# A gated delta-rule attention block on one core: weighted k, token-major z, no identity product, small scaling products on GpSimd, new orders

## The chip, the cores and the metric

The kernel runs on one core of a Trainium2 chip. The core has a matrix engine (TensorE, PE in the profile), a vector engine (VectorE, DVE), a scalar engine (ScalarE, ACT), a general engine (GpSimd, POOL) and a queue engine that issues the DMAs (SyncE, SP). Each takes its own instructions strictly in the order in which they are written, and they wait for each other with semaphores. The metric is the device time of one execution in microseconds (us). It is quoted as a median over executions.

## The reference

One transformer layer: a modulated layer norm, linear attention with a gated delta rule, and a small mixture of experts. The change lies almost wholly in the attention. For each of 8 batches and 16 key heads (128 pairs, called steps) there are two value heads and four chunks of 128 tokens. The reference writes it in chunks of 64; the kernel works in chunks of 128. Cut to what matters:

```python
mixed = silu(conv4(x @ W.T))        # q, k: 16 heads of 128; v: 32 heads of 128; z beside them, without conv
q, k = l2norm(q), l2norm(k)          # x / (|x| + 1e-6)
beta, g = sigmoid(b), cumsum(-exp(A_log) * softplus(a + dt_bias))   # per token and value head
decay = where(tril, exp(g[:, None] - g[None, :]), 0)
A = -where(strict_tril, (k*beta) @ k.T * decay, 0)
T = inverse(eye - A)                 # per chunk and value head
for each chunk:                      # state is 128 x 128 per value head, 0 at first
    v_new = T @ v_beta - (T @ (k_beta * exp(g))) @ state
    out   = (q * exp(g)) @ state + tril(q @ k.T * decay) @ v_new
    state = state * exp(g_last) + (k * exp(g_last - g)).T @ v_new
h = out * rsqrt(mean(out*out) + 1e-6)
y = (norm_weight * h * silu(z)) @ W_out.T
```

## The kernel before

Three stages follow each other: layer norm and gates, attention, experts. The attention stage holds 128 steps, one for each pair of batch and key head. Within a step everything is 128 partitions wide; `U` = 8 is four chunks times two value heads.

The work of a step is cut into named tasks. Each engine has a string (`PE_ORDER`, `ACT_ORDER`, `DVE_ORDER`, `POOL_ORDER`) that lists its tasks for one iteration of the steady loop. `P3@4` means: task P number 3, of the step four after the iteration's own number. An iteration so holds tasks of five steps (a software pipeline), and each step passes through five iterations. The orders alone set what stands behind what on an engine; a task waits on semaphores for what it reads and for the buffers it writes.

The tasks that matter here, in a step's own sequence:

- P0 to P11 (L658): the projections, six tiles (k, q, two of v, two of z) of two half products each, 128x512 float32. C copies a tile from PSUM with the last tap as scale (ACT L886), T adds the other three taps (DVE L1018). SK, SQ and SV are silu. Z is silu of the z tiles, straight from PSUM (ACT L891).
- KT, QT, KN, QN: transposes of k and q, their squares (ACT) and the sums of squares (DVE L1024, L1028). PW takes the root (POOL L1199). SM0 to SM3 and SN0 to SN2 (DVE L1034 to L1060) make the scales from it, each on 8 or 4 elements per partition: `neg_n`, `inv` (the reciprocal), `cc`, `neg_c`, `w_c`, `q_s2`, `q_s`.
- GL and GE: `low` = row of g plus a 0 or -1e30 mask (POOL L1194), and its exponential (ACT L924). KK (PE) is k.k and k.q, GA (DVE L1072, 8 instructions) multiplies it by `neg_c` and the decay. SL (POOL L1203) writes -1 into the diagonal, AR and AL split the matrix into bf16 parts, AB (DVE L1078) copies its diagonal blocks to `a_bd`.
- L, M, q, y, X, XB, Y: six levels of a blockwise inverse in bf16. On each level PE makes a product M, DVE masks it (q), DVE transposes `y_h` (X L1102), ACT and POOL both copy the transposed tile into `x_bd` (XB, ACT L936 and POOL L1225), PE makes Y from both, DVE adds (y L1093). Then come s, XD, Q6, `p` (copies `p_h` to bf16, DVE L1113), Z6, YC, XC: the last doubling.
- D, F, RL, G, v, W, IV: a refinement of the inverse. F is DVE L1118, RL is POOL L1217, v copies `g_t`. W adds up the refined inverse in PSUM; it begins with a product by the identity that puts `x_dn` there (L793). IV copies it out (ACT L966).
- VT and VK bring v to token order. Then for each chunk n the recurrence: KS (k times state), RR (DVE L1129), TR (the inverse times that), VX copies TR (ACT L979), VW multiplies TR by `w_c` (DVE L1140), U is k times `vw` (L826, one product for both heads), ST makes the new state (DVE), SD is the decayed state (POOL L1239), O is the output, OT copies it, OQ sums its squares (ACT).
- OS0, OS1 (DVE), OP (POOL: power -0.5 L1244, one product L1247) and ON (POOL L1253) normalise the output; ON on PE transposes it, HT multiplies it by `norm_w` and the transposed z (DVE L1164), OY is the output projection (L868) and YA adds it into `y_acc` (DVE L1170).

The banks `p_out0` and `p_out1` are shared by KT/QT, KK, VT, D, G, W, ON and OY, so each of these waits until the one before it was read.

## Time and profile before

| what | us |
| --- | --- |
| median of three runs | 4832.42 |
| lowest and highest | 4830.36, 4836.11 |
| span of the profiled execution | 4831.3 |
| attention, first to last SL task (128 steps) | 137.6 to 4593.3 |
| one step in the steady loop | 35.08 |

The span is 1.1 us under the median, so nothing of size lies outside it. The step time is the distance between the first and the last SL instruction over 127. What an engine does in a step repeats in every other one, so one step read closely stands for 128.

### The profile page before, as it was taken

The page shows a single profiled execution, that of the slowest core. Times are in us where ns is not written, and L with a number is a line of the kernel's source. Part 1 is how long each engine was busy: PE and PEld are TensorE (multiplying, and loading weights), DVE is VectorE, ACT ScalarE, POOL GpSimd, SP SyncE. Part 2 cuts the span into 40 slices and gives each one's busy share as a digit, 9 for nine tenths or more (in the row PEclk, how much of TensorE's full clock was granted, in tenths as well). Part 3 has the DMA queues.
Part 4 walks back from the last instruction along what each step waited for, and adds up shares of the span by engine and source line. Part 5 has one row for each costly group of instructions (what it writes and reads, how often), then busy time and mean ns, then how long its engine had stood idle before and what let it go on. Part 6 is the DMA issues. An engine that isn't in the chain of part 4 may idle for free. (4 is left out here: it accounts for less than half of the span.)

```text
span 4831.3 us, 132942 instructions
## 1 busy us (share of the span) xinstructions
PE 4671.0 (97%) x38533; PEld 3195.1 (66%) x38788; DVE 4411.5 (91%) x9152; ACT 3467.6 (72%) x8336; POOL 2743.0 (57%) x2329
## 2 busy tenths in 40 slices
PE   5899999999999999999999999999999999999978
PEld 3566666666666666666666666666666666666643
DVE  4899999999999999999999999999999999999953
ACT  3677777777777777777777777777777777777732
POOL 2456665656565665656566665656566665656520
PEclk7999999999999999999999999999999999999988
DMA  4222222222222222222222222222222222222122
GB/s 156 65 75 79 68 86 70 88 66 87 67 79 79 68 86 71 88 66 87 67 80 79 68 86 66 92 66 84 70 78 80 66 87 66 92 66 84 55 79 83
DMA packets 185165, 377.26 MB, mean 78 GB/s; under 512 B 86400, under 2 KB 95744, under 8 KB 184960
## 3 DMA queue, kind: packets, MB, share of 16 engines
q1 hardware_dynamic: 185088, 376.46, 24.7%
q14 instruction: 57, 0.47, 0.0%
...
## 5 line engine op out<-in xcount | busy, mean ns | idle before, releaser
L658 PE MATMUL p_proj<-hid,w_in 128*128 128x512 f32 x3072 | 1626.7, 612 | 30.0 <-POOL ident_h L1185 28.9
L1018 DVE SCALAR_TENSOR_TENSOR conv<-p_proj,taps,conv 128x509 f32<-128x509 f32 (+2 forms) x1536 | 1134.8, 739 | 48.2 <-ACT conv L886 34.9
L1199 POOL TENSOR_TENSOR root<-sums,half_pow 128x8 f32<-128x8 f32 x128 | 210.8, 1647 | 862.9 <-DVE sums L1028 843.9
L1225 POOL TENSOR_SCALAR_AFFINE_SELECT x_bd<-x_t 128x512 bf16<-128x512 bf16 x640 | 422.6, 660 | 213.5 <-DVE x_t L1102 211.2
L658 PEld LDWEIGHTS p_proj<-hid,w_in 128*128 128x128 f32 x3072 | 497.3, 192 | 55.1 <-POOL ident_h L1185 29.1
L1093 DVE TENSOR_TENSOR y_h<-p_lev,y_h 128x512 bf16<-128x512 f32 x640 | 440.2, 688 | 74.4 <-PE p_lev L725 74.4
L868 PE MATMUL p_out<-h_t,w_out 128*128 128x512 f32 x1024 | 476.5, 608 | 2.2 <-DVE h_t L1164 1.1
L936 ACT ACTIVATE x_bd<-x_t 64x512 bf16<-64x512 bf16 x640 | 397.7, 621 | 96.3 <-DVE x_t L1102 96.2
L1102 DVE STREAM_TRANSPOSE x_t<-y_h 128x512 bf16<-128x512 bf16 x640 | 450.3, 704 | 4.5
L1072 DVE SCALAR_TENSOR_TENSOR ga<-p_out,neg_c,dec 128x256 f32<-128x256 f32 x1024 | 412.9, 477 | 35.4 <-ACT dec L924 34.8
L886 ACT ACTIVATE conv<-p_proj,taps 128x512 f32<-128x512 f32 x512 | 351.7, 687 | 121.9 <-PE p_proj L658 119.3
L1085 DVE TENSOR_TENSOR q_h<-p_lev,consts 128x512 bf16<-128x512 f32 x640 | 429.6, 671 | 3.8 <-PE p_lev L718 3.8
L979 ACT ACTIVATE vx<-p_b 128x256 f32<-128x256 f32 x512 | 197.9, 386 | 285.8 <-PE p_b L816 161.4
L1217 POOL TENSOR_TENSOR r_lo<-resid 128x1024 bf16<-128x1024 f32 x128 | 242.3, 1893 | 247.9 <-DVE resid L1118 247.9
L838 PE MATMUL p_b<-vx,ga 128*128 128x128 f32 x2048 | 375.1, 275 | 0.0
L868 PEld LDWEIGHTS p_out<-h_t,w_out 128*128 128x128 f32 x1024 | 184.6, 190 | 285.0 <-DVE ga L1072 147.9
L725 PEld LDWEIGHTS p_lev<-q_h,x_bd 128*128 128x128 bf16 x5120 | 216.5, 97 | 213.5 <-issue 101.5
L985 ACT ACTIVATE o_tok<-p_b 128x256 f32<-128x256 f32 x512 | 194.1, 379 | 199.5 <-PE p_b L838 196.4
L718 PEld LDWEIGHTS p_lev<-y_h,a_bd 128*128 128x128 bf16 x5120 | 222.7, 98 | 152.1 <-issue 84.2
L1232 POOL TENSOR_TENSOR q_dec<-kq,e_row 128x512 f32<-128x512 f32 x256 | 320.0, 1271 | 0.0
L924 ACT ACTIVATE dec<-low,g_neg 128x128 f32<-128x128 f32 x1024 | 313.3, 388 | 1.6
L1244 POOL TENSOR_TENSOR o_sc<-o_sc,neg_half 128x8 f32<-128x8 f32 x128 | 211.4, 1651 | 168.9 <-DVE o_sc L1159 168.9
...
## 6 DMA issues: line engine op xcount, KB each, us to landing
w_in<-in_w_in SPq DMA_DIRECT2D x128, 768.0 KB, 6.3
g_row<-rows_scratch SPq DMA_DIRECT2D x128, 512.0 KB, 3.2
hid<-h_scratch SPq DMA_DIRECT2D x128, 512.0 KB, 7.4
e_row<-exp_rows_scratch SPq DMA_DIRECT2D x128, 512.0 KB, 5.3
w_out<-in_w_out SPq DMA_DIRECT2D x128, 256.5 KB, 2.7
...
```

What stands on the lines that cost most here:

```text
L658: last = pe.matmul(p_proj[tile % 2][:], w_in[p][:, kt, tile * P:(tile + 1) * P], hid[p][:, kt, :], start=(kt == 0), stop=(kt == KT - 1))
L838: last = pe.matmul(p_b[:, at], ga[p][:, n * HD + h, 1, :], vx[:, h, :], start=(n == 0), stop=True)
L868: last = pe.matmul(p_out[n][:], w_out[p][:, h * D + n * P:h * D + (n + 1) * P], h_t[:, :, h, :], start=(h == 0), stop=(h == HD - 1))
L886: act.activation(conv[:, n, :], p_proj[n % 2][:], ACT.Copy, scale=taps[p][:, n, PAD:PAD + 1])\
L936: act.activation(x_bd[0:HB, :, 0:HB], x_t[0:HB], ACT.Copy).then_inc(s["xbd"], 1)
L1018: dve.scalar_tensor_tensor(conv[:, tile, late:], p_proj[tile % 2][:, 0:S - late], taps[p][:, tile, j:j + 1], conv[:, tile, late:], ALU.mul ...
L1072: last = dve.scalar_tensor_tensor(ga[p][:, u], kk, neg_c[p][:, n, h:h + 1], each(dec[:, u, :], 2), ALU.mult, ALU.mult)
L1085: dve.tensor_tensor(q_h[:], levels(), each(const["mask"][:, n * HB:(n + 1) * HB], U), ALU.mult)\
L1093: dve.tensor_tensor(y_h[:], levels(), y_h[:], ALU.add).then_inc(s["y_done"], 1)
L1102: dve.transpose(x_t[:].rearrange("p u f -> p (u f)"), y_h[:].rearrange("p u f -> p (u f)"))\
L1225: pool.affine_select(x_bd[:, :, HB:P], x_t[:], [[0, U], [0, HB]], ALU.is_ge, zero, base=-HB, channel_multiplier=1).then_inc(s["xbd_low"], 1)
L1232: last = pool.tensor_tensor(q_dec[p][:, :, h, :], kq[p][:, :, 1, :], e_row[p][:].rearrange("p (c h) i -> p c h i", h=HD)[:, :, h, :], ALU. ...
```

## The change

- **Weighted k.** VW is gone. A new POOL task KW multiplies the token-major k by `w_c` once for three chunks and two heads (128x768) into `k_w`. U now is two products, one for each head, of `k_w` with `vx`; it waits for VX where it waited for VW.
- **No identity product.** W no longer begins with the product by `ident_h`. IV adds `x_dn` as it reads PSUM, and stands on DVE; it was a copy on ACT.
- **Token-major z.** P8 to P11 take the hidden tile as the stationary operand, so z comes out with tokens on partitions; each is two products of 256 columns, where there was one of 512. POOL multiplies the normalised output by z (a second 128x1024 product in ON), and HT becomes a scaled copy on ACT.
- **Scaling products on GpSimd.** SM0, SM2, SM3, SN0 to SN2, OS0 and OS1 move from DVE to POOL as parts of PW, SC, SN and OP. The reciprocal stays on DVE (SI), so POOL hands over to DVE and back between PW and SC.
- GL is an affine select instead of an addition with a mask. The copy to `p_h` moves from DVE to ACT (PH). The scale of the output's squares (1/128 ahead of squaring) goes into OQ. `g_col` holds minus beta, by one more constant in an instruction of the first stage, so `neg_c` needs no sign of its own. The bank releases that PE waits for follow the new sequence.
- All four orders are new. Projections run three steps ahead, no longer four.

```diff
-                    last = pe.matmul(p_proj[tile % 2][:], w_in[p][:, kt, tile * P:(tile + 1) * P], hid[p][:, kt, :],
-                                     start=(kt == 0), stop=(kt == KT - 1))
+                    if tile < 4:
+                        last = pe.matmul(p_proj[tile % 2][:], w_in[p][:, kt, tile * P:(tile + 1) * P], hid[p][:, kt, :],
+                                         start=(kt == 0), stop=(kt == KT - 1))
+                    else:
+                        c = n - 4 * KT
+                        for k in range(KT):
+                            last = pe.matmul(p_proj[tile % 2][:, kt * HD * DH:(kt + 1) * HD * DH],
+                                             hid[p][:, k, c * CH:(c + 1) * CH], w_in[p][:, k, 4 * P:6 * P],
+                                             start=(k == 0), stop=(k == KT - 1))
...
-                    pe.matmul(p_out[n][:], ident_h[:], quarter(x_dn, n).rearrange("p a i -> p (a i)"),
-                              start=True, stop=False)
...
                 elif name == "U":
-                    t.wait(pe, "vw_done", n + 1)
+                    t.wait(pe, "vx_done", n + 1)
                     if n == 0:
-                        t.wait(pe, "k_tok_done")
+                        t.wait(pe, "kw_done")
...
-                    pe.matmul(p_a[:, HD * DH:2 * HD * DH], k_tok[p][:, n, :], vw[:].rearrange("p h f -> p (h f)"),
-                              start=True, stop=True).then_inc(s["u_mm"], 1)
+                    for h in range(HD):
+                        last = pe.matmul(p_a[:, (HD + h) * DH:(HD + h + 1) * DH], k_w[p][:, n, h, :], vx[:, h, :],
+                                         start=True, stop=True)
+                    last.then_inc(s["u_mm"], 1)
...
+                elif name == "HT":
+                    t.wait(act, "on_mm", n + 1)
+                    t.wait(act, "y_out", back=1)
+                    act.activation(cols(h_t, n), bank(n), ACT.Copy, scale=const["norm_w"]).then_inc(s["h_done"], 1)
...
+                elif name == "IV":
+                    t.wait(dve, "w_mm", n + 1)
+                    t.wait(dve, "x12")
+                    t.wait(dve, "tr_mm", back=2)
+                    dve.tensor_tensor(quarter(inv_t[p], n), bank(n), quarter(x_dn, n), ALU.add).then_inc(s["inv_done"], 1)
...
-                    pool.tensor_tensor(low[:], g_row[p][:], each(const["bound"], U), ALU.add).then_inc(s["g_low"], 1)
+                    pool.affine_select(low[:], g_row[p][:], [[0, U], [1, CH]], ALU.is_ge, far_below, base=0,
+                                       channel_multiplier=-1).then_inc(s["g_low"], 1)
...
                     pool.tensor_tensor(root[:], sums[:], half_pow[:], ALU.pow).then_inc(s["rooted"], 1)
+                    t.wait(pool, "rooted")
...
+                    pool.tensor_scalar(neg_n[p][:], root[:], 1e-6, -1.0, ALU.add, ALU.mult).then_inc(s["scaled"], 1)
+                elif name == "SC":
...
+                    pool.tensor_tensor(cc[:], inv_k, minus_beta, ALU.mult).then_inc(s["scaled"], 1)
...
+                    pool.tensor_tensor(neg_c[p][:], cc[:], inv_k, ALU.mult).then_inc(s["scaled"], 1)
...
+                elif name == "KW":
+                    t.wait(pool, "k_tok_done")
+                    t.wait(pool, "w_scaled")
+                    t.wait(pool, "u_mm", back=2)
+                    pool.tensor_tensor(k_w[p][:], k_tok[p][:, 0:NC - 1].unsqueeze(2).to_broadcast([P, NC - 1, HD, DH]),
+                                       w_c[p][:, 0:NC - 1].unsqueeze(3).to_broadcast([P, NC - 1, HD, DH]), ALU.mult)\
+                        .then_inc(s["kw_done"], 1)
...
                     pool.tensor_tensor(o, o, scale, ALU.mult).then_inc(s["o_nrm"], 1)
+                    t.wait(pool, "o_nrm", 1)
+                    t.wait(pool, "z_done")
+                    pool.tensor_tensor(o, o, z_t[p][:].rearrange("p c h f -> p (c h) f"), ALU.mult).then_inc(s["o_nrm"], 1)
```

The orders, first on POOL, from the refinement's `r_lo` (RL) to the first `x_bd` copy of the next iteration. Before:

```order
L1217 TENSOR_TENSOR r_lo<-resid 128x1024
...
L1203 AFFINE_SELECT ga0<-ga0 128x8x128
L1244 TENSOR_TENSOR o_sc<-o_sc,neg_half 128x8
...
L1247 TENSOR_TENSOR o_sc<-o_sc,q_s0 128x8
...
L1225 AFFINE_SELECT x_bd<-x_t 128x8x64
...
L1253 TENSOR_TENSOR o_tok0<-o_tok0,o_sc 128x1024
```

The same place of the changed kernel:

```order
L1204 TENSOR_TENSOR r_lo<-resid 128x1024
L1240 TENSOR_TENSOR o_sc<-o_ss,q_s21 128x8
...
L1243 TENSOR_SCALAR o_sc<-o_sc 128x8
L1245 TENSOR_TENSOR o_sc<-o_sc,neg_half 128x8
L1247 TENSOR_TENSOR o_sc<-o_sc,q_s1 128x8
...
L1190 AFFINE_SELECT ga1<-ga1 128x8x128
...
L1183 TENSOR_TENSOR w_c1<-neg_c1,g_col1 128x8
L1184 TENSOR_TENSOR q_s21<-inv 128x4
L1185 TENSOR_SCALAR q_s1<-inv 128x4
L1253 TENSOR_TENSOR o_tok1<-o_tok1,o_sc 128x1024
L1256 TENSOR_TENSOR o_tok1<-o_tok1,z_t1 128x1024
...
L1212 AFFINE_SELECT x_bd<-x_t 128x8x64
```

The normalising power now stands ahead of the select on `ga`, three small products follow that, and both products on `o_tok` stand ahead of the first `x_bd` copy, where the one product stood behind it.

On POOL between the last two `x_bd` copies of the levels (levels 4 and 5), before:

```order
L1225 AFFINE_SELECT x_bd<-x_t 128x8x64
...
L1209 TENSOR_TENSOR a_rest<-ga1 128x1024
...
L1239 TENSOR_TENSOR state_dec<-state0,g_exp0 128x256
L1213 TENSOR_TENSOR a_lo<-a_rest 128x1024
...
L1225 AFFINE_SELECT x_bd<-x_t 128x8x64
```

And in the changed kernel:

```order
L1212 AFFINE_SELECT x_bd<-x_t 128x8x64
...
L1219 TENSOR_TENSOR q_dec0<-kq0,e_row0 128x4x128 x2
...
L1226 TENSOR_TENSOR k_w0<-k_tok0,w_c0 128x768
...
L1212 AFFINE_SELECT x_bd<-x_t 128x8x64
```

The two splits and the decayed state have moved up, and the two `q_dec` products and the new weighted k stand ahead of the fifth copy.

On DVE at the end of the GA instructions, before:

```order
L1072 SCALAR_TENSOR_TENSOR ga1<-p_out1,neg_c1,dec 128x256 x4
L1018 SCALAR_TENSOR_TENSOR conv<-p_proj1,taps1,conv 128x509
L1170 SCALAR_TENSOR_TENSOR y_acc<-y_acc,w_out0,p_out0 128x512
L1156 TENSOR_TENSOR o_sc<-o_ss,q_s21 128x8
L1078 CAST a_bd<-ga1 64x8x64 x2
L1159 TENSOR_SCALAR o_sc<-o_sc 128x8
```

And in the changed kernel:

```order
L1055 SCALAR_TENSOR_TENSOR ga1<-p_out1,neg_c1,dec 128x256 x4
L1029 SCALAR_TENSOR_TENSOR conv<-p_proj1,taps1,conv 128x510
L1029 SCALAR_TENSOR_TENSOR conv<-p_proj1,taps1,conv 128x511
...
L1131 SCALAR_TENSOR_TENSOR y_acc<-y_acc,w_out0,p_out0 128x512
L1061 CAST a_bd<-ga1 64x8x64 x2
...
L1131 SCALAR_TENSOR_TENSOR y_acc<-y_acc,w_out0,p_out1 128x512
L1102 TENSOR_TENSOR inv_t0<-p_out0,x_dn 128x512
```

The small products are gone, both additions into `y_acc` stand around the casts to `a_bd`, and the addition that makes the inverse follows.

## Rows read from the trace of the kernel before

**Rows 1.** The page: busy time of the engines, us and share of the span.

```profile
PE 4671.0 (97%) x38533; PEld 3195.1 (66%) x38788; DVE 4411.5 (91%) x9152; ACT 3467.6 (72%) x8336; POOL 2743.0 (57%) x2329
```

**Rows 2.** Windows: stretch, length, busy time of PE, PEld, DVE, ACT, POOL; clock.

```profile
1000.00:4000.00 3000.00, 2975.42 (x25302) 2060.47 (x25471) 2860.75 (x5992) 2260.40 (x5482) 1811.72 (x1535) 1.00 0.24 76
```

**Rows 3.** The line of SL: count, duration, start of the first and the last.

```profile
L1203 POOL TENSOR_SCALAR_AFFINE_SELECT ga<-ga x128: 1096/1097/1097, 137.6 to 4593.3; 128x1024 f32<-128x1024 f32 x128
```

**Rows 4.** Waits of DVE, 1500 to 3800 us: total, times, longest.

```profile
DVE y_h L1093 <- PE p_lev L725: 35.8, 65, 1.1
DVE ga L1072 <- ACT dec L924: 18.0, 66, 0.3
```

**Rows 5.** Groups on DVE, 1500 to 3800 us: count, busy us, mean ns, idle before.

```profile
L1164 DVE SCALAR_TENSOR_TENSOR h_t<-p_out,norm_w,z_t 128x512 f32<-128x512 f32 x132 | 98.6, 747 | 2.9
...
L1118 DVE TENSOR_TENSOR resid<-p_out,consts 128x512 f32<-128x512 f32 x132 | 90.9, 688 | 0.0
...
L1140 DVE TENSOR_TENSOR vw<-p_b,w_c 128x256 f32<-128x256 f32 x196 | 81.5, 416 | 3.5
...
L1078 DVE CAST a_bd<-ga 64x512 bf16<-64x512 f32 x132 | 55.3, 419 | 2.1
...
L1113 DVE CAST p_h<-p_lev 64x512 bf16<-64x512 f32 x65 | 45.1, 694 | 2.0
...
L1034 DVE TENSOR_SCALAR neg_n<-root 128x8 f32<-128x8 f32 x66 | 10.8, 163 | 0.0
```

**Rows 6.** Groups on POOL, the same stretch and columns.

```profile
L1232 POOL TENSOR_TENSOR q_dec<-kq,e_row 128x512 f32<-128x512 f32 x130 | 162.5, 1271 | 0.0
...
L1194 POOL TENSOR_TENSOR low<-g_row,consts 128x1024 f32<-128x1024 f32 x66 | 155.9, 2362 | 0.0
...
L1239 POOL TENSOR_TENSOR state_dec<-state,g_exp 128x256 f32<-128x256 f32 x131 | 80.4, 614 | 43.0 <-DMA g_exp<-gates_scratch 43.0
```

**Rows 7.** Groups on ACT, the same stretch and columns.

```profile
L886 ACT ACTIVATE conv<-p_proj,taps 128x512 f32<-128x512 f32 x261 | 179.3, 687 | 45.7 <-PE p_proj L658 45.7
...
L966 ACT ACTIVATE inv_t<-p_out 128x512 f32<-128x512 f32 x131 | 76.8, 586 | 100.1 <-PE p_out L798 100.1
...
L940 ACT ACTIVATE x_dn<-p_tr 128x1024 bf16<-128x1024 bf16 x65 | 67.4, 1037 | 0.0
```

**Rows 8.** Timeline of POOL: start us, us, instruction, idle before and its releaser.

```profile
2026.36 1.65 POOL L1199 TENSOR_TENSOR root<-sums,half_pow 128x8 f32<-128x8 f32 x1 [6.69 <-DVE sums L1028]
2029.99 1.89 POOL L1217 TENSOR_TENSOR r_lo<-resid 128x1024 bf16<-128x1024 f32 x1 [1.98 <-DVE resid L1118]
2033.59 1.10 POOL L1203 TENSOR_SCALAR_AFFINE_SELECT ga<-ga 128x1024 f32<-128x1024 f32 x1 [1.71 <-DVE ga L1072]
2035.98 1.65 POOL L1244 TENSOR_TENSOR o_sc<-o_sc,neg_half 128x8 f32<-128x8 f32 x1 [1.30 <-DVE o_sc L1159]
2037.71 0.20 POOL L1247 TENSOR_TENSOR o_sc<-o_sc,q_s 128x8 f32<-128x8 f32 x1
2038.62 0.67 POOL L1225 TENSOR_SCALAR_AFFINE_SELECT x_bd<-x_t 128x512 bf16<-128x512 bf16 x1 [0.70 <-DVE x_t L1102]
2039.25 1.90 POOL L1253 TENSOR_TENSOR o_tok<-o_tok,o_sc 128x1024 f32<-128x1024 f32 x1
```

**Rows 9.** Timeline of DVE, the casts to `a_bd` of the same step, same columns.

```profile
2034.83 0.87 DVE L1078 CAST a_bd<-ga 64x512 bf16<-64x512 f32 x2
```

**Rows 10.** Timeline of PE: start us, us from first to last, instruction, count.

```profile
2008.63 0.68 PE L803 MATMUL p_a<-state,kq 128*128 128x256 f32 x2
2009.36 0.22 PE L796 MATMUL p_out<-x_dn,r_lo 128*128 128x128 bf16 x1
...
2012.54 1.02 PE L658 MATMUL p_proj<-hid,w_in 128*128 128x512 f32 x2
2013.39 0.40 PE L718 MATMUL p_lev<-y_h,a_bd 128*128 128x64 bf16 x8
2013.63 0.68 PE L803 MATMUL p_a<-state,kq 128*128 128x256 f32 x2
```

More of the change, by code:

```diff
@@ L426, in attention @@
         k_tok, v_tok = two("k_tok", [P, NC, DH]), two("v_tok", [P, NC, HD, DH])
+        k_w = two("k_w", [P, NC - 1, HD, DH])
         eye_h, ident_h = sb("eye_h", [P, HB], BF), sb("ident_h", [P, P], BF)
@@ L913, in emit @@
                     t.wait(act, "kt_mm")
-                    t.wait(act, "u_mm", back=2)
+                    t.wait(act, "kw_done", back=2)
                     act.activation(k_tok[p][:], bank(0), ACT.Copy).then_inc(s["k_tok_done"], 1)
@@ L939, in emit @@
                     t.wait(act, "w_mm", back=1)
+                    t.wait(act, "inv_done", back=1)
                     act.activation(x_dn[:].rearrange("p u i -> p (u i)"), p_tr_h, ACT.Copy).then_inc(s["xdn"], 1)
@@ L946, in emit @@
                        .then_inc(s["y21"], 1)
+                elif name == "PH":
+                    t.wait(act, "q6_mm")
+                    t.wait(act, "z6_mm", back=1)
+                    act.activation(p_h[HB:P], p_lev[HB:P, :].rearrange("p (u f) -> p u f", f=HB), ACT.Copy).then_inc(s["p6_done"], 1)
                 elif name == "XC":
@@ L962, in emit @@
                     last.then_inc(s["v_tok_done"], 1)
-                elif name == "IV":
-                    t.wait(act, "w_mm", n + 1)
-                    t.wait(act, "tr_mm", back=2)
-                    act.activation(quarter(inv_t[p], n), bank(n), ACT.Copy).then_inc(s["inv_done"], 1)
                 elif name == "v":
@@ L993, in emit @@
                     for h in range(HD):
-                        last = act.activation(o_junk[:, h, :], o_tok[p][:, n, h, :], ACT.Square, accum_out=o_ss[:, n, h:h + 1])
+                        last = act.activation(o_junk[:, h, :], o_tok[p][:, n, h, :], ACT.Square, scale=1.0 / DH,
+                                              accum_out=o_ss[:, n, h:h + 1])
                     last.then_inc(s["osq"], 1)
@@ L1062, in emit @@
+                elif name == "SI":
+                    t.wait(dve, "scaled", 1)
+                    t.wait(dve, "scaled", back=1)
+                    t.wait(dve, "q_scaled", back=1)
+                    dve.reciprocal(inv[:], neg_n[p][:]).then_inc(s["inverted"], 1)
                 elif name == "GA":
@@ L1109, in emit @@
                     dve.tensor_copy(y_dn[half(n - 10), :, half(n - 10)], y_h[half(n - 10)]).then_inc(s["ydn"], 1)
-                elif name == "p":
-                    t.wait(dve, "q6_mm")
-                    t.wait(dve, "z6_mm", back=1)
-                    dve.tensor_copy(p_h[HB:P], levels()[HB:P]).then_inc(s["p6_done"], 1)
                 elif name == "F":
@@ L1242, in emit @@
                 elif name == "OP":
+                    t.wait(pool, "osq")
+                    t.wait(pool, "q_scaled")
+                    t.wait(pool, "o_nrm", 1, back=1)
+                    pool.tensor_tensor(o_sc[:], o_ss[:], over(q_s2[p][:], [P, NC, HD]), ALU.mult).then_inc(s["osm"], 1)
+                    t.wait(pool, "osm", 1)
+                    pool.sem_inc(passed, 1)
+                    pool.tensor_scalar(o_sc[:], o_sc[:], 1e-6, None, ALU.add).then_inc(s["osm"], 1)
                     t.wait(pool, "osm")
```

189 lines of the change are left out of this document (76 added, 113 removed), and 3 rows, old and new, of the table DVE_ORDER.

## The prediction

> **What bounds the kernel now.** I read the page's busy times first [rows 1], then the busy times of a long stretch of the attention, the distance between steps, and last the waits. The reader sees in the page that TensorE and DVE are both above 90%, and that the granted clock is full through the attention (1.00 between 1000 and 4000 us, the 2.4 GHz level [rows 2]), so no part of the answer is a clock. The 128 steps run from 137.6 to 4593.3 us by their SL instruction, (4593.3 - 137.6) / 127 = 35.08 us each [rows 3]. The other 376 us (norms, filling, draining, experts) are not touched, save one constant. So the question is what a step costs.
>
> DVE is busy 2860.75 of 3000 us, 95.4%, or 33.5 us a step [rows 2]. Its waits are 35.8 us and 18.0 us in 66 steps, 0.8 us a step [rows 4]; what remains is short gaps between instructions. DVE is full. TensorE shows 99%, but a matmul's shown time overlaps the next one's, so I count columns. One projection product (two passes of 512 columns) is followed 0.85 us later (2012.54 to 2013.39) and eight bf16 products of 64 columns 0.24 us later (2013.39 to 2013.63) [rows 10]: two clock cycles per float32 column and pass, one per bf16 column. By the code a step has 30,200 float32 columns (both passes; 25.2 us) and 16,400 bf16 ones (6.8 us): 32.0 us, and with some 0.02 us at each of 60 changes of group 33.2 us. So TensorE is 95% full as well, and stands 1.9 us of each step behind others. ACT is busy 26.4 us of a step and POOL 21.2 us [rows 2]. Two engines are at their limit, and a change has to relieve both.
>
> **The change part by part**, per step of 35.08 us.
>
> DVE loses VW (3 x 0.416), HT (2 x 0.747), the copy to `p_h` (0.694) and eight small products (8 x 0.16, by the row of `neg_n`): 4.7 us [rows 5]. It gains IV twice. No row has DVE adding a bf16 tile to PSUM; `resid` adds a constant to the same bank in 0.688 [rows 5], so 1.4 us. Net -3.3 us; since instructions overlap by 0.08 us in the trace, some -3.0 in pace. DVE needs about 30.4 us and is no longer the bound.
>
> TensorE loses the identity product twice. Between KS at 2008.63 and the rest of W at 2009.36 lie 0.73 us, of which KS takes 0.43 [rows 10]; 1024 bf16 columns at one per cycle are 0.43 us a step. U keeps its columns. The z products keep theirs as well, with more weight loads; KS streams 256 columns a pass with a load behind each, so I take +0.05 us, between 0 and 0.3. TensorE then needs 32.8 us.
>
> ACT loses the copies of IV (2 x 0.586) and gains HT as scaled copies (2 x 0.687, by the scaled copy of `conv`) and PH (about 0.59): +0.8 us, 27.2 in all [rows 7].
>
> POOL: GL becomes a select, 2.362 to 1.10 [rows 6, 8]: -1.27. The product of `o_tok` and z reads two full tiles, like `low` at 2.362 and not like the product with a repeated scale at 1.90 [rows 6, 8]: +2.36, at least 1.90. KW has 768 elements: by `state_dec`, which also reads a repeated scale, (0.614 - 0.203) / 256 x 768 + 0.203 = 1.44 us; by `q_dec` 1.81 us [rows 6]. I take 1.45. The eight small products: the one row of such a product on POOL is 0.20, the power on as many elements is 1.65 [rows 8]. They are plain products and additions, so 0.2 each and 0.1 between dependent ones: +2.4, with 3 x 1.45 more at the far end if the three with constants cost as much as the power. Sum +4.9, POOL at 26 us of 35. That is no bound by total, but it is one by sequence.
>
> **The loop through POOL.** Before, POOL idles 6.7, 2.0, 1.7 and 1.3 us around the root, `r_lo`, the select and the power [rows 8]; nothing waits long for it. In the new order all that lies in one row, and behind it stands the first `x_bd` copy, which level 1 (Y1) on TensorE needs. Y1 leads through the levels back to the sums. I follow the loop from Y1 to the next Y1:
>
> - Y1 to the end of the transposes XD on TensorE: the products that stand between in the order, 16.4 us.
> - Then ACT: the rest of PH and `x_dn` (1.04) [rows 7], the squares of q (0.55), and DVE's sum (0.65), with handovers: 2.9 us.
> - POOL: root 1.65, `neg_n`, DVE's reciprocal, `cc`, `neg_c` with five handovers 1.35, `r_lo` 1.9, the output's scale 2.55 (0.2 + 0.2 + 1.65 + 0.2 and waits), the select 1.1 and its start 0.05, three small ones 0.75, two products on `o_tok` 4.3, the copy 0.65, and 0.1 to TensorE: 14.4 us [rows 6, 8].
>
> That is 33.7 us. The fifth copy stands behind `q_dec` and KW (2.5 + 1.45), and X5 is ready 3.5 us after X4, so Y5 comes some 0.3 us late; part of this is hidden because PH stands behind another wait on ACT. The output projection OY needs `ga` half by half; with `neg_c` at 21.9 us of the iteration, GA ends at 23.6 and 25.2, when TensorE arrives. L needs the cast behind SL at about 28.4, and TensorE comes at 29.0. W1 and v1 are within 0.2 us of each other. I take 34.0 us a step: above TensorE's 32.8, and a gain of 1.08 us.
>
> 128 x 1.08 = 138 us, so 4832 - 138 = 4694. The pipeline spans as much time from a step's projection to its last addition as 3.8 iterations, where it was 4.0; that is a few us in draining. **Forecast 4690 us.**
>
> **The rivals.**
>
> 1. TensorE becomes the bound: the loop is shorter than I make it, since small POOL products follow each other closely or the z product is 1.90. Then 32.8 us and the usual late handovers of 0.4: 33.2 us, 4832 - 128 x 1.88 = 4590. For it speaks that DVE has 3 us to spare, so fewer things come late; against it that seven rows of POOL add up to nearly a step.
>
> 2. DVE's casts and POOL get into each other's way. The cast to `a_bd` from SBUF takes 0.419 us where the cast of as many elements from PSUM takes 0.694 [rows 5], so it runs in a faster mode. Before, POOL idled while it ran: the casts run from 2034.83 to 2035.70 [rows 9], POOL is idle from 2034.69 to 2035.98 [rows 8]. Now three small products and the first of the long ones stand there. If the two take turns, the two casts (2 x 0.42) enter POOL's row once, +0.75 us: 34.75 us, 4790.
>
> The Trainium skill, "SBUF — State Buffer", section "Who interferes with whom", states that a DVE copy or cast in a two-port mode and a GpSimd instruction exclude each other for the whole of the one that came first. By that rule the casts' 0.84 us would be in the loop; no row of before has the two side by side, so the trace neither agrees nor disagrees.
>
> 3. Slower: a small instruction with constants costs on POOL what the power costs. `neg_n` and the `+ 1e-6` lie in the loop, and `q_s` as well. At 1.65 us each this is 3 x 1.45 = 4.35 us a step: 38.3 us, 4832 + 128 x 3.2 = 5240. It decides from 0.36 us more each on (1.08 / 3); beyond that the kernel is slower. Against it: the product on 8 elements takes 0.20 [rows 8], so starting an instruction is cheap, and the 1.65 belong to the power.
>
> 4. No change: the losses on other handovers eat the 1.08 us. Between 4823 and 4842.
>
> **How the numbers follow.** Forecast (33.6 to 34.4 us a step, 4640 to 4745) 0.53; TensorE alone 0.16; casts in the way 0.15; no change 0.05; slower 0.11. The predicted time is the first's. The range leaves out the slower case and the end of the first rival: 4595 to 4815. About 0.2% is what a measurement of this kernel can tell from no change: faster 0.84, same 0.05, slower 0.11.
>
> **What would show it.** Steps 34.0 us apart; DVE busy near 88% with long idle stretches before the reciprocal and GA; POOL with no idle time from the root to the first `x_bd` copy, and TensorE waiting for that copy in front of Y1. KW at 1.45 and the second product on `o_tok` at 2.36. Were TensorE to wait at OY or L instead, the GA part of the loop would be wrong; were it to wait nowhere, rival 1 holds. A POOL instruction with constants above 0.5 us, or casts to `a_bd` longer than 0.42, would show rivals 3 and 2. What would make it wrong outright is a handover that I have not followed: four orders are new, and I have followed one loop.

## The result, and the profile after

The changed kernel takes 4816.11 us (median of 4, 4812.11 to 4817.64) against 4832.06 us before (4830.36 to 4836.11), a ratio of 0.9961 with a 95% interval of 0.9948 to 0.9974. It is faster by 0.4%, where 2.9% was forecast, and the time lies 1.1 us above the range. The direction was right, the size was not.

The page and the window of 1000 to 4000 us after the change, with the columns of [rows 1] and [rows 2]:

```profile
PE 4662.8 (97%) x40324; PEld 3437.2 (71%) x40324; DVE 4132.1 (86%) x7616; ACT 3620.5 (75%) x8462; POOL 3318.0 (69%) x3609
1000.00:4000.00 3000.00, 2983.08 (x26662) 2228.88 (x26661) 2690.74 (x4989) 2374.32 (x5591) 2212.31 (x2409) 1.00 0.25 77
```

DVE's busy time fell from 2860.75 to 2690.74 us of 3000 [rows 2], 33.5 to 31.3 us a step: 2.1 us, where the forecast took 3.0. The durations of its instructions do add up to 3.3 us less a step, as forecast, but neighbours overlap less than before. POOL went from 21.2 to 25.7. So the work moved as planned, and the pace hardly did. The line of the SL instruction, with its first and last start, answers [rows 3]:

```profile
L1190 POOL TENSOR_SCALAR_AFFINE_SELECT ga<-ga x128: 1098/1098/1101, 141.0 to 4575.1; 128x1024 f32<-128x1024 f32 x128
```

(4575.1 - 141.0) / 127 = 34.91 us a step: 0.17 less than before, not 1.08. Next the waits, 1500 to 3800 us (total, times, longest), which answer [rows 4]:

```profile
POOL root L1162 <- DVE sums L1039: 339.8, 65, 5.2
ACT vx L985 <- PE p_b L822: 126.1, 198, 0.9
DVE y_h L1076 <- PE p_lev L733: 70.4, 66, 1.1
PEld p_lev L733 <- ACT x_bd L941: 43.3, 66, 0.7
```

POOL's wait in front of the root is the only one above 2 us. No product on TensorE has a named wait, but weight loads, which run ahead of the products, have: the one for Y1 (L733) waits 0.7 us for the first copy to `x_bd`. POOL's timeline of one step, which answers [rows 8]:

```profile
2021.53 1.67 POOL L1162 TENSOR_TENSOR root<-sums,half_pow 128x8 f32<-128x8 f32 x1 [5.22 <-DVE sums L1039]
2023.48 0.20 POOL L1167 TENSOR_SCALAR neg_n<-root 128x8 f32<-128x8 f32 x1 [0.28 <-POOL root L1162]
2024.09 0.20 POOL L1174 TENSOR_TENSOR cc<-inv,g_col 128x8 f32<-128x8 f32 x1 [0.41 <-DVE inv L1044]
2024.46 0.20 POOL L1177 TENSOR_TENSOR neg_c<-cc,inv 128x8 f32<-128x8 f32 x1 [0.17 <-POOL cc L1174]
...
2029.14 1.10 POOL L1190 TENSOR_SCALAR_AFFINE_SELECT ga<-ga 128x1024 f32<-128x1024 f32 x1
2030.21 0.20 POOL L1183 TENSOR_TENSOR w_c<-neg_c,g_col 128x8 f32<-128x8 f32 x1
2030.37 0.38 POOL L1184 TENSOR_TENSOR q_s<-inv 128x4 f32<-128x4 f32 x1
2030.84 0.40 POOL L1185 TENSOR_SCALAR q_s<-inv 128x4 f32<-128x4 f32 x1
2031.32 1.90 POOL L1253 TENSOR_TENSOR o_tok<-o_tok,o_sc 128x1024 f32<-128x1024 f32 x1
2033.30 2.37 POOL L1256 TENSOR_TENSOR o_tok<-o_tok,z_t 128x1024 f32<-128x1024 f32 x1
2035.62 0.66 POOL L1212 TENSOR_SCALAR_AFFINE_SELECT x_bd<-x_t 128x512 bf16<-128x512 bf16 x1
```

The row that was foreseen is there, from the root to the first copy to `x_bd`, with no idle time save in the handovers behind the root and one of 0.19 us beside the output's scale. TensorE, ahead of and at Y1 (L733), and at the end of the levels one step earlier (L739 is XD):

```profile
2001.69 0.39 PE L733 MATMUL p_lev<-q_h,x_bd 128*128 128x64 bf16 x8
2018.26 0.61 PE L739 MATMUL p_tr<-ident_h,y_dn 128*128 128x128 bf16 x8
2035.79 0.65 PE L857 MATMUL p_out<-consts,o_tok 128*128 128x128 f32 x4
2036.38 0.39 PE L733 MATMUL p_lev<-q_h,x_bd 128*128 128x64 bf16 x8
```

The loop of the forecast, measured: Y1 to the end of XD (the next group starts at 2018.70), 2001.69 to 2018.70, 17.0 us (forecast 16.4); on to the root at 2021.53, 2.8 us (2.9); POOL and the handover to Y1 at 2036.38, 14.85 us (14.4). Together 34.7. The steps alternate between a shorter and a longer one; the next has 17.2, 2.8 and 15.0 us, 35.1, by the same rows one step on. The mean is the step of 34.9. Taken alone this looks as if the forecast had only been short in its sum. The experiments show that this is half of it.

POOL's row meets TensorE's once more, directly ahead of Y1. The transposes ON of the output (L857) stand there and wait for the product with z. In the nine steps from 2000 to 2290 us they start 0.12 to 0.14 us after that product ends (here 2033.30 + 2.37 = 2035.67 and 2035.79), and Y1 starts 0.10 us after the copy. The forecast's list has the copy alone.

### The profile page after: what moved, and what is told of

The parts are those of the page before. It is cut to its first block and busy times, and to the rows that moved or that the text cites. A ratio compares the mean times of both kernels' runs of the same rounds, so it can differ in the third digit from the quotient of the medians.

```text
span 4815.4 us, 136820 instructions
## 1 busy us (share of the span) xinstructions
PE 4662.8 (97%) x40324; PEld 3437.2 (71%) x40324; DVE 4132.1 (86%) x7616; ACT 3620.5 (75%) x8462; POOL 3318.0 (69%) x3609
## 5 line engine op out<-in xcount | busy, mean ns | idle before, releaser
L1029 DVE SCALAR_TENSOR_TENSOR conv<-p_proj,taps,conv 128x509 f32<-128x509 f32 (+2 forms) x1536 | 1133.4, 738 | 43.4 <-ACT conv L891 34.1
L659 PE MATMUL p_proj<-hid,w_in 128*128 128x512 f32 x2048 | 1080.3, 610 | 30.6 <-POOL ident_h L1146 28.7
L664 PE MATMUL p_proj<-w_in,hid 128*128 128x256 f32 x2048 | 547.8, 390 | 9.5 <-DVE conv L1029 9.5
L941 ACT ACTIVATE x_bd<-x_t 64x512 bf16<-64x512 bf16 x640 | 399.0, 623 | 97.3 <-DVE x_t L1085 80.6
L664 PEld LDWEIGHTS p_proj<-w_in,hid 128*128 128x128 f32 x2048 | 371.3, 191 | 50.7 <-DVE conv L1029 10.6
L659 PEld LDWEIGHTS p_proj<-hid,w_in 128*128 128x128 f32 x2048 | 320.5, 192 | 41.2 <-POOL ident_h L1146 29.0
L843 PE MATMUL p_b<-state,q_dec 128*128 128x128 f32 x1536 | 318.0, 289 | 0.5 <-ACT vx L985 0.5
L833 PEld LDWEIGHTS p_a<-vx,k_w 128*128 128x128 f32 x1536 | 221.7, 191 | 129.0 <-ACT vx L985 62.8
L733 PEld LDWEIGHTS p_lev<-q_h,x_bd 128*128 128x128 bf16 x5120 | 210.2, 97 | 143.6 <-ACT x_bd L941 91.4
```

The lines of the kernel that those rows point to most:

```text
L659: last = pe.matmul(p_proj[tile % 2][:], w_in[p][:, kt, tile * P:(tile + 1) * P], hid[p][:, kt, :], start=(kt == 0), stop=(kt == KT - 1))
L664: last = pe.matmul(p_proj[tile % 2][:, kt * HD * DH:(kt + 1) * HD * DH], hid[p][:, k, c * CH:(c + 1) * CH], w_in[p][:, k, 4 * P:6 * P], st ...
L941: act.activation(x_bd[0:HB, :, 0:HB], x_t[0:HB], ACT.Copy).then_inc(s["xbd"], 1)
L1029: dve.scalar_tensor_tensor(conv[:, tile, late:], p_proj[tile % 2][:, 0:S - late], taps[p][:, tile, j:j + 1], conv[:, tile, late:], ALU.mul ...
```

## The experiments

All are edits of the changed kernel, except one of the kernel before. A row is from here on also a stretch of one engine's order in which one instruction follows directly on the other. Steps are read from the line of the SL instruction (first and last start, over 127); added lines shift its number. The kernel before, measured beside them, took 4832.6 to 4834.3 us. q, h, j, l, m and k leave a part of the computation out: they test rows and are no versions of the kernel. The first table adds work, the second takes it away:

| kernel | what is different | SL first, last | step us | median us | ratio to before |
| --- | --- | --- | --- | --- | --- |
| changed | | 141.0, 4575.1 | 34.91 | 4816.11 | 0.9961 |
| b_spare_idle | POOL +1.27 outside its row | 137.4, 4571.0 | 34.91 | 4812.82 | 0.9960 |
| c_spare_chain | POOL +1.27 in its row | 137.7, 4706.0 | 35.97 | 4951.55 | 1.0250 |
| d_kt_twice | TensorE +0.43 between Y1 and XD | 141.2, 4627.5 | 35.33 | 4867.48 | 1.0071 |
| e_kk1_twice | TensorE +0.43 between XD and Y1 | 138.3, 4600.3 | 35.13 | 4839.72 | 1.0013 |

| kernel | what is taken away | SL first, last | step us | median us | ratio to before |
| --- | --- | --- | --- | --- | --- |
| f3_split | POOL 1.9 of its row (TensorE +0.47 behind Y2) | 140.8, 4574.3 | 34.91 | 4813.56 | 0.9958 |
| q_half_z | POOL 1.1 of its row, nothing else | 138.3, 4530.1 | 34.58 | 4767.32 | 0.9862 |
| h_no_p5 | TensorE 0.86 between Y1 and XD | 139.3, 4573.3 | 34.91 | 4810.60 | 0.9951 |
| j_no_p7 | TensorE 0.86 between XD and Y1 | 140.5, 4571.6 | 34.89 | 4809.89 | 0.9952 |
| l_taps_copy_only | DVE 0.65, copy ahead of `k_w` | 137.9, 4570.7 | 34.90 | 4809.83 | 0.9950 |
| m_no_copy_move | TensorE 0.86, DVE 0.65 | 140.4, 4573.9 | 34.91 | 4814.34 | 0.9959 |
| k_three_rows | all three of h, l and m | 141.2, 4543.1 | 34.66 | 4778.61 | 0.9882 |

### Is the loop through POOL real? b, c, d, e

The same spare product is put outside the row and into it.

```diff
+        spare = sb("spare", [P, 512])
...
+                elif name == "SX":
+                    pool.tensor_tensor(spare[:], const["all"][:, 0:512], const["all"][:, 256:768], ALU.mult)
...
 b:  ... XB5@2 SX@2 PW@3 SC@3 ...
 c:  ... SL@3 SX@3 SN@3
```

> The changed kernel with one more POOL instruction a step that nobody reads: a product of 128x512 float32 with two full operands (1.28 us by the q_dec row) directly ahead of the root, where POOL sits idle for 5.2 us. Theory L: no change, 4816 us within 8, since it lies outside the loop. Theory T: no change. A third one, that POOL is short of time in total: 128 x 1.28 = 164 us more, 4980.

> The same spare product of 1.28 us, now behind the select on ga and ahead of the small products, within the row from the root to the first x_bd copy. Theory L: every step 1.2 to 1.3 us longer, 4816 + 160 = 4976 us. Theory T: most of it goes into POOL's own waits, at most 50 us more, 4866.

b costs nothing (4812.82, interval 0.9946 to 0.9974), c costs 1.06 us a step (4951.55, 1.0232 to 1.0267). So POOL's busy total is no limit, and its row is one, as the forecast said. c came 0.2 us under the product's duration. Its trace explains most of that: the spare product now stands beside the casts of DVE, and the three small products behind it take 0.98 us (2011.35 to 2012.33), where they take 1.11 in the changed kernel (2030.21 to 2031.32).

TensorE's transposes of k are made twice (d), then half of the products KK (e):

```diff
 d: -                    for c in range(NC):
    +                    for c in (*range(NC), *range(NC)):
 e: -                    for c in (0, 1):
    +                    for c in (0, 1, 0, 1) if n else (0, 1):
```

> The changed kernel with the four transposes of k made twice (the second time over the first, the same values): 0.44 us more on TensorE in the part of its order between Y1 and XD, which lies in the loop. Theory L and theory T both: 128 x 0.44 = 56 us more, 4872 us. If neither holds and TensorE has room there, 4816.

> The changed kernel with the second half of KK made twice (same values): 0.43 us more on TensorE in the part of its order behind XD, beside POOL's row. Theory L: TensorE's waits there (0.4 before ON, 0.2 at O, 0.2 at M1 and KK) take it up, and only what delays GA counts: between 0 and 25 us more, 4816 to 4841. Theory T: the whole of it, 128 x 0.43 = 55 us, 4871.

0.43 us more between Y1 and XD lengthens the step by 0.41 (1.0054 to 1.0087). 0.43 us more between XD and Y1, where by the forecast TensorE only waits for POOL, still lengthens it by 0.22 (1.0004 to 1.0023), the far end of what had been expected if TensorE waits there. The expected reason, a later GA, isn't it: from the root to the end of the first copy POOL takes 14.68 us (2032.29 to 2046.97), as before (14.75). TensorE itself is late at ON and Y1:

```profile
2043.98 2.36 POOL L1256 TENSOR_TENSOR o_tok<-o_tok,z_t 128x1024 f32<-128x1024 f32 x1
2046.96 0.60 PE L857 MATMUL p_out<-consts,o_tok 128*128 128x128 f32 x4
2047.41 0.41 PE L733 MATMUL p_lev<-q_h,x_bd 128*128 128x64 bf16 x8
```

ON starts 0.62 us after the product with z ends (0.26 in every other step), not 0.13. That is the first number that spoke against the forecast: behind XD an addition of 0.43 us finds 0.21 us of room, not the 1.2 us of 34.0 against 32.8.

### The casts and POOL: a, g

SN, the three small products behind SL, is moved behind the first copy, which should shorten POOL's row by 1.1 us.

```diff
-POOL_ORDER = ("ON@0 XB1@2 AR@2 XB2@2 ... SL@3 SN@3")
+POOL_ORDER = ("ON@0 XB1@2 SN@2 AR@2 XB2@2 ... SL@3")
```

> The changed kernel with one task moved: POOL's three small products on w_c, q_s2 and q_s (1.1 us from the end of the select on ga to the start of the product on o_tok in its trace) stand behind the first x_bd copy and no longer ahead of both products on o_tok. Theory L (a step is as long as the loop through POOL: TensorE from Y1 to XD, ACT and DVE to the sums, POOL from the root to the first x_bd copy, 34.91 us in all): the loop gets 1.1 us shorter, and since TensorE shows only some 1.0 us of waits in a step, the step falls to about 34.0 us: 4816 - 115 = 4700 us, between 4675 and 4725. Theory T (TensorE is full as it is, and POOL only just keeps up): no change, 4816 us within 10.

It took 5177.49 us, a ratio of 1.0715 (1.0698 to 1.0733), and neither expectation was near. The rows: both casts to `a_bd` on DVE with POOL beside them, and TensorE's wait (L is L721):

```profile
2023.14 4.60 DVE L1061 CAST a_bd<-ga 64x512 bf16<-64x512 f32 x2
2023.08 1.90 POOL L1253 TENSOR_TENSOR o_tok<-o_tok,o_sc 128x1024 f32<-128x1024 f32 x1
2025.06 2.40 POOL L1256 TENSOR_TENSOR o_tok<-o_tok,z_t 128x1024 f32<-128x1024 f32 x1
PE p_lev L721 <- DVE a_bd L1061: 154.5, 60, 2.6
L1061 DVE CAST a_bd<-ga x256: 406/2116/2469, 138.7 to 4936.0; 64x512 bf16<-64x512 f32 x128
```

The casts take 4.60 us where they took 0.87 [rows 9]: the first ends about with the one POOL product, the second about with the other. In the changed kernel SN stands just there, and the casts are short:

```profile
2030.27 0.87 DVE L1061 CAST a_bd<-ga 64x512 bf16<-64x512 f32 x2
```

There it is POOL that pays: L1184 and L1185 take 0.38 and 0.40 us beside the casts, 0.20 and 0.24 when they are elsewhere, in a_sn_late:

```profile
L1184 POOL TENSOR_TENSOR q_s<-inv x128: 201/202/204, 143.3 to 4942.2; 128x4 f32<-128x4 f32 x128
```

To tell the exclusion from the new place of SN, g keeps the order of a and lets POOL wait for the casts before it goes on.

```diff
-POOL_ORDER = ("ON@0 XB1@2 SN@2 AR@2 ... SL@3")
+POOL_ORDER = ("ON@0 XB1@2 SN@2 AR@2 ... SL@3 WA@3")
+                elif name == "WA":
+                    t.wait(pool, "abd")
+                    pool.sem_inc(passed, 1)
```

> As a_sn_late, and POOL now waits for DVE's two casts to a_bd before it starts the products on o_tok. In a_sn_late the casts took 2.3 us each where they take 0.42, and L on TensorE waited 2.6 us for them. If the cause is that a cast cannot run beside a long POOL product (theory P), the wait gives the casts back their 0.42 us; POOL then loses some 0.95 us to the wait where it gained 1.1 us from the three small ones, and the time is 4816 - 15, between 4785 and 4825. If the loss in a_sn_late comes from the later w_c (KW, the gate columns' DMA) it stays near 5177.

4834.53 us (0.9996 to 1.0015), 343 us less than a by one wait: the cost of a was the overlap itself. It is 10 us above the range expected, 35.12 us a step. The casts are back at 0.42, and POOL waits for them and for their start:

```profile
POOL o_tok L1256 <- DVE a_bd L1061: 91.4, 66, 1.6
```

91.4 / 66 = 1.4 us, where 0.95 had been expected and SN had filled 1.1. So SN behind SL is a good filler, and nothing is to be had by moving it.

### A shorter row on POOL: f2, f3, q

f2 splits the two products on `o_tok`: the one with the scale before the first copy, the one with z behind it. TensorE's transposes of the first half (ON0) stand behind Y2, as in f3.

```diff
-POOL_ORDER = ("ON@0 XB1@2 AR@2 XB2@2 SD1@1 ... XB5@2 PW@3 SC@3 RL@2 OP@1 SL@3 SN@3")
+POOL_ORDER = ("XB1@2 ON1@0 XB2@2 SD1@1 ... AR@2 ... XB5@2 AL@2 PW@3 SC@3 RL@2 OP@1 SL@3 SN@3 ON0@1")
```

> The changed kernel with POOL's two products on o_tok apart: the scaling one where it was, the one with z behind the first x_bd copy; the three small ones stay behind the select, so that the casts to a_bd still meet only short instructions. TensorE transposes the output's first half later (behind Y2). a_rest and a_lo move down, a_lo behind the fifth copy and behind the copies to y_dn. Theory L: 2.37 us less in the loop, so another bound ends the gain: TensorE has about 1.0 us of waits, thus 33.9 to 34.2 us a step and 4690 to 4725 us. Theory T: 4816 us within 10. Theory P has nothing against it, unless the z product meets a cast or copy (+2 us a step, 5070).

5009.38 us (1.0347 to 1.0382), 36.47 us a step, a miss for a reason of its own. ScalarE's silu of z waits until the late product has read the z buffer, and TensorE's projections wait for the bank:

```profile
ACT z_t L896 <- POOL o_tok L1260: 110.5, 64, 1.8
PEld p_proj L659 <- ACT z_t L896: 96.3, 64, 1.6
```

f3 turns it round: the product with z first, in the old place, that with the scale behind the copy. The transposes ON0 stand behind Y2 here too.

```diff
-POOL_ORDER = ("ON@0 XB1@2 ...")
+POOL_ORDER = ("XB1@2 ON0@0 XB2@2 ... AR@2 ... AL@2 ... SL@3 SN@3 ON1@1")
-PE_ORDER = ("... TR1@1 Y2@2 P1@3 ... O0@2 ON0@1 Y1@3 G1@2")
+PE_ORDER = ("... TR1@1 Y2@2 ON0@0 P1@3 ... O0@2 Y1@3 G1@2")
```

> As f2_split, whose z product came so late that ACT waited for z's buffer. Now the product with z comes first, where the scaling one was (1.9 against 2.37 us), and the scaling product stands behind the first x_bd copy; ACT's z waits for the product with z alone. Theory L: 1.9 us less in the loop, then TensorE's own bound of about 34 us: 33.9 to 34.3 us a step, 4690 to 4740 us. If ACT still waits for z or TensorE for the transposes of the output, between 4740 and 4816. Theory T: 4816.

4813.56 us (0.9944 to 0.9971), 34.91 a step: 1.9 us out of the row and nothing gained. But it puts four transposes, 0.47 us, between Y1 and XD, where d had shown that an addition of 0.43 us counts almost in full. q takes 1.1 us out of the row and moves nothing.

```diff
-                    pool.tensor_tensor(o, o, z_t[p][:].rearrange("p c h f -> p (c h) f"), ALU.mult).then_inc(s["o_nrm"], 1)
+                    half, z = slice(0, U // 2), z_t[p][:].rearrange("p c h f -> p (c h) f")
+                    pool.tensor_tensor(o[:, half], o[:, half], z[:, half], ALU.mult).then_inc(s["o_nrm"], 1)
```

> The changed kernel with GpSimd's product with z over half of its 1024 columns (the other half is left out), 1.2 us less in the row between the sum and the first copy to x_bd; nothing else is moved, TensorE's order neither. The forecast's one loop: 1.2 us a step less, 4665. Theory R for the other half of the step: ScalarE's own first copy to x_bd ends only 0.3 us ahead of GpSimd's, behind v_tok and vx, which wait for TensorE; so 0.2 to 0.3 us a step, 4778 to 4791.

4767.32 us (0.9845 to 0.9878), 34.58 a step: 0.33 us of 1.1. What comes last now of the two copies is ScalarE's (L941), behind `v_tok` and `vx`, which waits for TensorE:

```profile
2014.82 0.38 ACT L985 ACTIVATE vx<-p_b 128x256 f32<-128x256 f32 x1 [0.86 <-PE p_b L822]
2015.30 0.84 ACT L969 ACTIVATE v_tok<-p_out,neg_n 128x256 f32<-128x256 f32 x2
2016.03 0.62 ACT L941 ACTIVATE x_bd<-x_t 64x512 bf16<-64x512 bf16 x1
2015.33 0.67 POOL L1212 TENSOR_SCALAR_AFFINE_SELECT x_bd<-x_t 128x512 bf16<-128x512 bf16 x1
2016.70 0.41 PE L733 MATMUL p_lev<-q_h,x_bd 128*128 128x64 bf16 x8
PEld p_lev L733 <- ACT x_bd L941: 43.9, 67, 0.7
```

POOL's copy ends at 2016.00, ScalarE's at 2016.65, and Y1 starts at 2016.70. In the changed kernel ScalarE's copy ends at 2035.97 and POOL's at 2036.28, so 0.3 us was all that could be won. TensorE's own row ends there too: ON starts at 2016.25, 1.0 us after the product with z and no longer held by it, and Y1 follows 0.45 us later, for 0.43 us of columns. Which of the two set the step in q isn't shown. So f3 gained its 0.3 us at Y1 and lost it to the 0.47 behind Y2: in both kernels Y3 starts 10.1 us after `y0`.

### Less between Y1 and XD: h, j, l, m, k

P5 is left out (h), or P7, which stands behind XD (j).

```diff
 h: +                    if tile == 2 and kt == 1:
    +                        return
 j: +                    if tile == 3 and kt == 1:
    +                        return
```

> The changed kernel without the second half product of tile 2 of the projections (P5, 0.86 us; v is then computed from half of the hidden vector). It stands in the part of TensorE's order that is in the loop. Theory L: the whole of it comes off the step, as far as the copies and levels beside it allow: 0.6 to 0.86 us, 4706 to 4740 us. Theory T: 0.86 us as well, 4706.

> The changed kernel without the second half product of tile 3 (P7, 0.86 us; the second v head from half of the hidden vector), which stands behind Z6 in the part of TensorE's order that runs beside POOL's row. Theory L: TensorE only waits longer for POOL, 0 to 0.2 us off the step, 4790 to 4816 us. Theory T: 0.86 us, 4706.

j gains nothing that can be told from zero, as expected behind XD. h should have gained 0.6 to 0.86 us a step and gained nothing either (0.9936 to 0.9966). Its rows around y5 (the last addition of the levels), TensorE, POOL and DVE:

```profile
2048.18 0.60 PE L677 MATMUL p_out<-consts,kq 128*128 128x128 f32 x4
2049.49 0.39 PE L735 MATMUL p_lev<-q_h,x_bd 128*128 128x64 bf16 x8 [0.72 <-ACT x_bd L943]
2047.31 1.47 POOL L1228 TENSOR_TENSOR k_w<-k_tok,w_c 128x768 f32<-128x768 f32 x1
2048.73 0.66 POOL L1214 TENSOR_SCALAR_AFFINE_SELECT x_bd<-x_t 128x512 bf16<-128x512 bf16 x1
2049.11 0.74 DVE L1031 SCALAR_TENSOR_TENSOR conv<-p_proj,taps,conv 128x511 f32<-128x511 f32 x1
2049.92 0.69 DVE L1078 TENSOR_TENSOR y_h<-p_lev,y_h 128x512 bf16<-128x512 f32 x1
```

TensorE now waits in front of Y5 (L735). The wait is put down to ScalarE, but the copy that ends last is POOL's: 2048.73 + 0.66 = 2049.39, and it stands behind the product to `k_w`, which the change has put there. And DVE is busy until 2049.85 with the third tap of a projection, then makes y5 at 2049.92. So two more rows end at y5, on POOL and on DVE, each within 0.1 us of TensorE's. Three kernels cut them two and two and all together. The tap product T5 shrinks to 8 columns; the fifth copy goes ahead of `k_w`.

```diff
+                    end = late + 8 if n == 5 else S
-                    dve.scalar_tensor_tensor(conv[:, tile, late:], ...
+                    dve.scalar_tensor_tensor(conv[:, tile, late:end], ...
...
-POOL: XB4@2 QD@2 KW@2 XB5@2 PW@3      ACT: SK@3 VK1@2 XB5@2 KN@3
+POOL: XB4@2 QD@2 XB5@2 KW@2 PW@3      ACT: SK@3 XB5@2 VK1@2 KN@3
```

> The two edits of k_three_rows without the first: P5 is made as in the changed kernel, T5 covers 8 of 510 columns (the rest of that tap is left out), the fifth copy stands ahead of the k_w product. Theory R: TensorE's row to Y5 is as long as before, so 4805 to 4816. If VectorE's row alone set the start of y5: 0.65 us a step less, 4733.

> k_three_rows with the fifth copy left where the changed kernel has it, behind the k_w product: P5 is left out and T5 covers 8 of 510 columns. Theory R: GpSimd ends its copy 0.1 us before Y5 starts in the changed kernel, so all but 0.1 us stays, 4800 to 4816. If VectorE's row and TensorE's were the only ones: 4725 to 4745, as k_three_rows.

> The changed kernel with P5 left out (as in h_no_p5: one half of the projection's third tile is missing, so part of the computation is left out) and with two more edits: the tap product T5 on VectorE is made over 8 of its 510 columns (0.65 us less, the rest of that tap is left out), and the fifth copy to x_bd is put ahead of the k_w product on GpSimd and ahead of v_tok's second half on ScalarE. Theory R (three rows are level when y5 starts: TensorE from Y1 to Y5, VectorE without a gap from the state copy to y5, GpSimd's k_w product in front of the fifth copy): all three are cut now, TensorE by 0.86, GpSimd by 1.3, VectorE by 0.65, the least decides, so 0.6 to 0.65 us a step of 127, 4725 to 4745. Theory L of the forecast (one loop, through TensorE and GpSimd) would have given this already in h_no_p5, which it did not; theory B (TensorE bounds the whole step at 34.9): 4706 to 4745 in h_no_p5 too. If a fourth row is level with the three: 4800 to 4816.

With TensorE's row left (l) 4809.83 us, with POOL's copy left (m) 4814.34, with neither 4778.61 (0.9865 to 0.9898). l and m are what three level rows predict; that DVE's row binds as well has no run of its own with the other two cut. k is half right: y5 came 0.67 us earlier against `y0`, as expected, but the step only 0.25. The rest went to a fourth row, read from the traces; no run shortens it. ScalarE, from a copy that waits for TensorE to the squares of q, the changed kernel first:

```profile
2048.20 0.39 ACT L991 ACTIVATE o_tok<-p_b 128x256 f32<-128x256 f32 x1 [1.06 <-PE p_b L844]
...
2054.90 0.59 ACT L924 ACTIVATE squares<-p_out 128x512 f32<-128x512 f32 x1
```

and k_three_rows, with the wait of DVE for it:

```profile
2034.66 0.39 ACT L993 ACTIVATE o_tok<-p_b 128x256 f32<-128x256 f32 x1 [1.06 <-PE p_b L846]
...
2041.12 0.59 ACT L926 ACTIVATE squares<-p_out 128x512 f32<-128x512 f32 x1
DVE sums L1042 <- ACT squares L926: 41.0, 66, 0.6
```

From the copy to the squares it is 6.70 us before (2048.20 to 2054.90) and 6.46 us now, with the same eleven further instructions between them and no recorded wait; in the changed kernel small gaps are left (0.13 us ahead of `p_h`, which waits for TensorE's Q6), in k_three_rows that one is 0.03. The copy waits for a product that stands ahead of P5 on TensorE, so it doesn't move. So this row had some 0.25 us of slack, and 0.25 is what k gained.

### Was DVE the bound before? i

The kernel before loses the identity product and gains IV on DVE, as the change has it.

```diff
-ACT_ORDER: ... AO@2 v0@1 IV0@1 XB1@2 ... Z1@2 XB3@2 IV1@1 VK0@2 ...
+ACT_ORDER: ... AO@2 v0@1 XB1@2 ... Z1@2 XB3@2 VK0@2 ...
-DVE_ORDER: T10@3 y0@3 T11@3 X1@3 q1@3 ... VW1@2 ...
+DVE_ORDER: T10@3 y0@3 T11@3 X1@3 IV0@2 q1@3 ... VW1@2 IV1@2 ...
```

> The kernel before with one part of the change alone: no identity product, and the inverse is written by an addition on DVE and not by a copy on ACT. TensorE has 0.43 us less a step, DVE 1.2 us more. If DVE is what the kernel before is full of (95% busy, waits of 0.8 us a step), it costs 0.7 to 1.2 us a step: 4832 + 90 to 150, about 4950. If TensorE is the bound, it gains up to 55 us, 4777.

4900.85 us (1.0127 to 1.0161); its SL line:

```profile
L1203 POOL TENSOR_SCALAR_AFFINE_SELECT ga<-ga x128: 1096/1096/1098, 136.3 to 4657.9; 128x1024 f32<-128x1024 f32 x128
```

35.60 us a step, 0.52 more, with less work on TensorE and ScalarE and 1.3 more on DVE (2 x 0.663). The expected range began at 0.7. DVE's busy share went from 95.4 to 96.7% and its named waits from 0.9 to 0.6 us a step (58.5 us in 66 steps, 39.1 in 64). That agrees with DVE as what held the pace before, though not for the whole 1.3: waits and short gaps took part of it. The run can't tell DVE's total from the places that the two IV tasks got in its order.

## Where the prediction was right and where it failed

**The bound before: right.** DVE was full, the clock was not in it, and a step decides. Run i agrees, with less than was expected of it.

**The prices of instructions: right.** KW 1.47 (forecast 1.45, [rows 6]), the product with z 2.37 (2.36), the select in place of GL 1.09 (1.10), HT on ScalarE 0.68 (0.687), IV on DVE 0.69 (0.688), small instructions with constants 0.20 to 0.25 (0.2):

```profile
L1226 POOL TENSOR_TENSOR k_w<-k_tok,w_c 128x768 f32<-128x768 f32 x66 | 97.2, 1473 | 0.0
L1102 DVE TENSOR_TENSOR inv_t<-p_out,x_dn 128x512 f32<-128x512 f32 x132 | 91.3, 692 | 33.6 <-PE p_out L804 30.5
```

Rival 3 is dead by `neg_n` at 0.198.

**The signs, POOL's row without idle time in front of Y1 and TensorE held by it there: right.** The row's length was 14.85 and 15.0, not 14.4. Most of the 0.45 of the first is in the three small ones, 1.11 in place of 0.75: the two `q_s` instructions beside the casts take 0.78, without them 0.44.

**Rival 2, the casts: right as a mechanism, and small only by luck of the order.** The casts do stand beside POOL instructions, but beside two of 0.2 us. The price there is 0.34 us, not 0.75, and it is in POOL's row. With long products beside them it is 3.7 us of DVE's time and 2.84 us a step: the SL starts of a_sn_late run from 137.5 to 4932.7, 37.76 us apart. The Trainium skill, "SBUF — State Buffer", section "Who interferes with whom", says that a DVE cast in a two-port mode and a GpSimd instruction exclude each other for the whole of the one that came first; the durations in a_sn_late agree, where each cast lasts about as long as the product beside it.

**The loop: the terms that were mis-sized.** "Y1 to the end of the transposes XD on TensorE ... 16.4 us" measured 17.0 and 17.2, and POOL's 14.4 measured 14.85 and 15.0. The term for a late Y5, 0.3 us, was not there: Y5 follows 0.88 us after P5, for 0.85 us of columns. On the mean of two steps that is +0.7, +0.5 and -0.3, and -0.1 for ScalarE's and DVE's part, so 34.0 becomes 34.9 within rounding. The 16.4 was added up from columns and 0.02 us for each change of group. TensorE's rows in that stretch:

```profile
2045.31 1.10 PE L659 MATMUL p_proj<-hid,w_in 128*128 128x512 f32 x2
2046.25 0.61 PE L833 MATMUL p_a<-vx,k_w 128*128 128x128 f32 x4
2046.79 0.39 PE L733 MATMUL p_lev<-q_h,x_bd 128*128 128x64 bf16 x8
```

A projection product is followed after 0.94 us here (0.85 of columns), U after 0.54 (0.43). Part of that are handovers and not TensorE's own pace: the weight load for this U waits 0.24 us for `vx`. Over the step TensorE has 31.6 us of columns by the code and 3.3 us beside them. So the change's 0.43 us of columns went, and the excess grew from 3.1 to 3.3 us.

**The second failed step: "TensorE then needs 32.8 us".** No run shows that number, and the traces speak for more. The room of 0.21 us that e_kk1_twice found would put it at 34.7, but q_half_z does all of TensorE's work in 34.58 us a step. Closer is a sum over neighbours in TensorE's order. Eight pairs of groups lie further apart in the changed kernel than at their closest in seven kernels with the same order on TensorE (steps between 2000 and 2290 us), by 0.8 us together, half of it ahead of ON and Y1, where POOL holds it. Without that the step is 34.1 us, 2.5 above the columns, where the forecast had put 1.2 (60 x 0.02) and 0.05. That is an estimate, and handovers that are the same everywhere are still in it. So TensorE alone would have ended the gain at about the forecast's 34.0, and rival 1, "TensorE alone", at 33.2 us a step and 4590 us, was priced some 0.9 us a step too fast. [rows 10] gave little warning: of the 0.73 us between KS and the rest of W the columns of KS (0.43) and of one identity product (0.21) explain 0.64, and 0.09 was left, where I took 0.02.

**The third: one loop was followed.** "The fifth copy stands behind `q_dec` and KW ... so Y5 comes some 0.3 us late" named the second row and let it go. At ON and Y1 POOL's row holds TensorE twice. At y5 three rows end within 0.1 us of each other (TensorE's, DVE's, POOL's copy behind `k_w`), ScalarE's row to the squares is 0.25 us behind them, and at Y1 ScalarE's copy is 0.3 us behind POOL's. So even with the right price for each term the sum of one loop could not give the gain of an edit: h, l and m each take work out of the loop or a neighbour and gain nothing.

So of the expected 1.08 us 0.17 came. Of the missing 0.9 us q won back 0.33 when POOL's row was shortened; the other 0.6 no run won back. The estimate of 34.1 us for TensorE leaves 0.5 below the 34.58 of q, in small waits at other joints.

No version here that computes the whole layer beats the changed one by more than its measurement tells: f3_split is at 4813.56 and b_spare_idle at 4812.82. What stays open is whether an order exists that takes 0.3 us out of all rows at once. No run takes the parts of the change one by one on the changed kernel, so what each part brought or cost isn't shown either.
